# Self-edges of a graph counted with 25-column matmuls, and the 13 edge rows of histogram and ranking unrolled

## The reference

```python
x = x + attention(layernorm(x), rows=src, cols=dst)     # softmax over the edges of each src
x = x + experts(layernorm(x))
# graph attention: for each dst, softmax over its edges; one more self-edge per node is appended
src2 = concatenate([src, arange(n)]); dst2 = concatenate([dst, arange(n)])
h = gelu(gat(gelu(gat(layernorm(x), W0, src2, dst2)), W1, src2, dst2))
x = x + h; x = x + gated_experts(layernorm(x))
```

## Time and profile before

| | us |
|---|---|
| median of 3 runs | 4101.75 (4097.06 to 4112.96) |
| the profiled execution | 4131.15, its span 4129.2 |
| table "s": block A, B, C | 116 to 261, 261 to 410, 411 to 633 |
| table "d": block A, B, C | 636 to 752, 753 to 904, 905 to 1128 |
| all that follows | 1131 to 4129 |

### The profile page before, as it was taken

One profiled execution on the slowest core, in us unless ns is written; L12 is line 12 of the kernel. 1 busy time (PEld: TensorE's weight loads), 2 busy tenths in 40 slices (PEclk: granted clock), 3 DMA queues, 4 the chain that ended last, 5 costly groups with the idle time before them and its releaser, 6 DMA issues. The chain is left out here.

```text
span 4129.2 us, 64690 instructions
## 1 busy us (share of the span) xinstructions
PE 2505.8 (61%) x14572; PEld 1764.4 (43%) x14586; DVE 2269.1 (55%) x6592; ACT 1371.1 (33%) x4015; POOL 1731.6 (42%) x1826
## 2 busy tenths in 40 slices
PE   7569587586835454563799954344444445434399
PEld 4348124461223333343699952233322333323288
DVE  7857798667947676766311123444445444445542
ACT  2215581246846676431244421000000100000144
POOL 1510600013056666652122246566654656665411
PEclk9579795788966677675799976776777776677789
DMA  5148300561086666632222223333443333444200
GB/s 173 39 90 195 120 14 3 136 149 63 13 250 195 191 194 185 185 109 64 68 77 76 77 63 99 105 108 105 111 104 83 94 104 108 110 110 99 77 26 18
DMA packets 260802, 432.61 MB, mean 105 GB/s; under 512 B 101193, under 2 KB 185744, under 8 KB 259832
## 3 DMA queue, kind: packets, MB, share of 16 engines
q0 software_dynamic: 92912, 316.02, 26.5%
q1 hardware_dynamic: 124824, 108.37, 10.1%
q10 hardware_dynamic: 42992, 7.34, 1.0%
HBM read 378.79 MB, written 52.78 MB: 105 GB/s over the span
## 5 line engine op out<-in xcount | busy, mean ns | idle before, releaser
L1275 PE MATMUL gt_part<-gt_wv,all_ident 128*128 128x260 f32 x1648 | 566.8, 504 | 750.7 <-DVE gt_wv L1104 657.4
L1025 POOL DMA_INDIRECT gt_rows<-h_rows,gt_idx x824 | 789.0, 958 | 505.2 <-DVE gt_wv L1104 269.9
L1275 PEld LDWEIGHTS gt_part<-gt_wv,all_ident 128*128 128x128 f32 x1648 | 394.2, 252 | 923.3 <-DVE gt_wv L1104 721.7
L1025 POOL DMA_INDIRECT att_rows<-kv_rows,att_idx x412 | 425.0, 1031 | 385.4 <-issue 176.3
L1275 PE MATMUL att_part<-att_wv,all_ident 128*128 128x264 f32 x824 | 332.0, 572 | 351.3 <-ACT att_wv L1229 203.3
L1275 PEld LDWEIGHTS att_part<-att_wv,all_ident 128*128 128x128 f32 x824 | 221.0, 283 | 462.2 <-issue 336.2
L1229 ACT ACTIVATE att_wv<-att_rows,att_wv 128x32 f32<-128x32 f32 x1504 | 341.9, 308 | 88.5 <-issue 60.4
L1104 DVE TENSOR_TENSOR gt_wv<-gt_rows,gt_exps 128x1040 f32<-128x1040 f32 (+1 forms) x224 | 260.7, 1164 | 77.6 <-ACT gt_exps L1224 49.5
L1224 ACT ACTIVATE gt_exps<-gt_score 128x20 f32<-128x20 f32 (+1 forms) x224 | 42.5, 190 | 743.1 <-issue 395.4
L1224 ACT ACT_TABLE_LOAD x57 | 73.1, 1283 | 544.5 <-issue 544.2
L1123 DVE TENSOR_TENSOR gt_acc<-gt_acc,gt_part 128x260 f32 x224 | 95.1, 425 | 224.5 <-DMA qkv_x_all<-in_x 109.2
(11 more groups left out here) (536 smaller groups left out, 5299.9 us busy)
## 6 DMA issues: line engine op xcount, KB each, us to landing
ex_w<-in_W SPq DMA_DIRECT2D x16, 1024.0 KB, 6.4
ixbs_parts_bc<-key_parts_s SPq DMA_DIRECT2D x14, 1024.0 KB
ixbs_parts_bc<-key_parts_s SPq DMA_DIRECT2D x28, 512.0 KB
ixbd_parts_bc<-key_parts_d SPq DMA_DIRECT2D x14, 1024.0 KB
ixbd_parts_bc<-key_parts_d SPq DMA_DIRECT2D x28, 512.0 KB
gt_rows<-h_rows,gt_idx POOLq DMA_INDIRECT x824
kv_rows<-qk_kv_all SPq DMA_DIRECT2D x5, 1440.0 KB, 8.4
y_rows<-ex_y POOLq DMA_DIRECT2D x55, 128.0 KB, 2.0
```

Of the source, the lines that this page charges most:

```text
L1025: pool.indirect_dma_start(out=rows[:, k, r, :], out_offset=None, in_=table, in_offset=bass.IndirectOffsetOnAxis(ap=idx[:, k, r:r + 1], axi ...
L1275: last = pe.matmul(part[:, k, 0:h * av], c.ident[:, :], wv[:, k, first_wv + r, :, :].rearrange("p h f -> p (h f)"), start=(r == 0), stop=( ...
```

## The change

- Self-edges: ACT alone makes the one-hot, 25 `Square` instructions over 416 elements each, one for a tile number, and then 13 `Relu` (a row each). PE multiplies `oh_lo` with it into `node_loops`, 32 matmuls of 25 columns a row, each row 4 rows (`LOOP_LAG`) behind the histogram and the last 4 after the class sums. DVE cuts the counts into two digits (`loop_digits`, 5 small steps). In both tables POOL multiplies the digits with the one-hot of tiles (2 instructions, 128x625), PE puts them in the order of the table with 50 matmuls into `loops_ps`, ACT copies to `g.loops`.
- The DRAM table `loop_rows`, its stores, its fill and all 50 gathers of L753 are gone, with their waits.
- Block A's and block B's loops over rows are written out, all addresses constant; `load_low`, `load_key` and one-hots for row 13 are gone. SP's loop is written out too.
- `LEAST_ROUNDS` goes from 16 to 28. The first tile's largest degree is 35, so no round changes; but `sure_chunks(4)` goes from 2 to 5, so `attend` issues 4 index loads at once, not 2 and then 2 after reading the list.

```diff
-                    with dve.Fori(0, EU) as u:
+                    for u in range(EU):
                         one_hots(dve, u, ohs)
@@ block A, vector, after oh_val
+                    if count_loops:
+                        dve.wait_ge(loops_summed, EU)
+                        step(dve.tensor_copy(loops_i[:, 0, :], node_loops[:, :]))
+                        step(dve.tensor_single_scalar(loops_i[:, 1, :], loops_i[:, 0, :], LOOP_DIGIT - 1, ALU.bitwise_and))
+                        step(dve.tensor_single_scalar(loops_i[:, 2, :], loops_i[:, 0, :], 8, ALU.logical_shift_right))
+                        step(dve.tensor_copy(c.loop_digits[:, :, :], loops_i[:, 1:3, :]))
+                        dve.tensor_scalar(c.loop_digits[:, 1, :], c.loop_digits[:, 1, :], float(LOOP_DIGIT), None, ALU.mult).then_inc(loops_cut, 1)
@@ gpsimd
-                    if count_loops:
-                        with pool.Fori(0, EU) as u:
-                            pool.tensor_tensor(oh_loop[...], g.hi_c[...], c.iota_b[...], ALU.subtract).then_inc(loop_off, 1)
...
                     pool.partition_all_reduce(mdeg[:, :], sdeg[:, :], P, RMAX).then_inc(maxed, 1)
+                    if count_loops:
+                        pool.wait_ge(loops_cut, 1)
+                    for k in range(2):
+                        pool.tensor_tensor(loop_val[:, k, :, :], oh_tile[:, :, :], c.loop_digits[:, k, :].unsqueeze(2).to_broadcast([P, NT, NT]),
+                                           ALU.mult).then_inc(loops_valued, 1)
+                    pool.wait_ge(loops_valued, 2)
@@ scalar
+                        for t in range(NT):
+                            act.activation(oh_loop[:, :, :, t], g.hi_c[:, :, :, :].rearrange("p u x q -> p u (x q)"), ACT.Square, scale=-1.0,
+                                           bias=c.iota_f[:, LOOP_TILE + t:LOOP_TILE + t + 1]).then_inc(loop_squared, 1)
+                        act.wait_ge(loop_squared, NT)
+                        for u in range(EU):
+                            act.activation(oh_loop[:, u, :, :], oh_loop[:, u, :, :], ACT.Relu, scale=-1.0, bias=c.ones[:, 0:1]).then_inc(loop_ohs, 1)
...
+                    act.wait_ge(loops_placed, 1)
+                    act.activation(g.loops[:, :], loops_ps[:, :], ACT.Copy).then_inc(loops_ready, 1)
@@ tensor
+                    def loop_row(u):
+                        pe.wait_ge(loop_ohs, u + 1)
+                        for t in range(XC):
+                            last = pe.matmul(node_loops[:, :], oh_lo[:, u, t, :], oh_loop[:, u, t, :], start=(u == 0 and t == 0),
+                                             stop=(u == EU - 1 and t == XC - 1), skip_group_check=True)
+                        last.then_inc(loops_summed, 1)
-                    with pe.Fori(0, EU) as u:
+                    for u in range(EU):
                         pe.wait_ge(ohs, u * 2 + 2)
                         row(u)
+                        if count_loops and u >= LOOP_LAG:
+                            loop_row(u - LOOP_LAG)
@@ block B
-                row(0, 0, 0, True)
-                with eng.Fori(0, EU // 2) as i:
-                    for k in (1, 2):
-                        row(i * 2 + k, k % 2, i, False)
+                for u in range(EU):
+                    row(u, u % 2, u == 0)
...
-                            if x == 1:
+                            if x == 1 and u < last_u:
                                 low_one_hots(1 - uk, u + 1)
@@ block C, gpsimd
-                    for t in range(NT):
-                        pool.indirect_dma_start(out=g.loops[:, t:t + 1], out_offset=None, in_=loop_rows,
-                                                in_offset=bass.IndirectOffsetOnAxis(ap=g.order[:, t:t + 1], axis=0)).then_inc(loops_in, 16)
```

More of the change, by code:

```diff
@@ L425, in _ @@
                     act.wait_ge(lanes_set, 1)
[L426 to L431, removed]
+                    act.wait_ge(loops_placed, 1)
+                    act.activation(g.loops[:, :], loops_ps[:, :], ACT.Copy).then_inc(loops_ready, 1)
+                    act.wait_ge(loops_ready, 1)
                 @block.tensor
                 def _(pe):
[L435 to L448, removed]
+                    def loop_row(u):
[4 more added lines that the diff above has]
+                        last.then_inc(loops_summed, 1)
                     for b in range(2):
@@ L470, in _ @@
                     if count_loops:
-                        loop_rows(0, FIRST_LOOP_ROWS)
+                        for u in range(EU - LOOP_LAG, EU):
+                            loop_row(u)
                     pe.wait_ge(valued, 3)
@@ L477, in _ @@
                     last.then_inc(sums, 1)
-                    if count_loops:
-                        loop_rows(FIRST_LOOP_ROWS, EU)
-                        pe.wait_ge(loops_copied, 1)
-                        for t in range(EX):
-                            last = pe.matmul(loop_sums[:, :], c.ident[:, t * LOOP_TILE:t * LOOP_TILE + NT], loops_sb[:, t, :], start=(t == 0), stop=(t == EX - 1))
-                        last.then_inc(loops_joined, 1)
+                    pe.wait_ge(loops_valued, 2)
+                    for t in range(NT):
+                        for k in range(2):
+                            last = pe.matmul(loops_ps[:, :], oh_lane[:, t, :], loop_val[:, k, t, :],
+                                             start=(t == 0 and k == 0), stop=(t == NT - 1 and k == 1))
+                    last.then_inc(loops_placed, 1)
         with Mem(nc, f"ixb{g.name}") as b:
@@ L547, in _ @@
                                  entry[0:TAIL, 1, :]).then_inc(list_out, 16)
[L548 removed]
+                    for r in range(last_u):
                         sp.wait_ge(ohT_ready, r * 2 + 1)
[L550 removed]
+                        load_low(r + 1)
                         sp.wait_ge(ohT_ready, r * 2 + 2)
[L552 to L553 removed]
+                        load_key(r + 1)
                     sp.wait_ge(list_out, wins * 16 + 32)
                     sp.sem_inc(g.passed, 1)
[L556 to L557 removed]
                 @block.scalar
@@ L562, in _ @@
                     act.sem_inc(earlier_ready, 2)
-                    with act.Fori(0, EU) as u:
+                    for u in range(EU):
                         for x in range(EX):
@@ L624, in sum_places, with row @@
                                           pick[:, k, :, :, :].rearrange("p q r t -> p (q r) t"), AX.X, ALU.add).then_inc(reduced, 1)
-                    def row(u, uk, i, first):
+                    def row(u, uk, first):
                         for x in range(EX):
@@ L640, in _ @@
                     key_one_hots(0, 0)
-                    row_loop(dve, row)
+                    each_row(row)
                     for x in (2, 3):
```

56 lines of the change are left out of this document (16 added, 40 removed).

## The result

The kernel after takes 3977.44 us (median of 4 runs, 3973.43 to 3980.92) against 4102.26 (4097.06 to 4112.96): a ratio of 0.9692, 95% interval 0.9671 to 0.9714, 124.8 us less. I had forecast 3982.

What follows compares the result with a forecast made beforehand. Bounds: DVE in block A of "s", PE and DMA near their limits in B, DVE shut out by POOL's gathers in C. Savings 31.8 + 4.0 + 17.6 + 33.7 + 33.1 = 120; 4101.75 - 120 = 3982 us, range 3950 to 4032.

Steps and rivals of the forecast that it cites:

- Block A: One-hots, histogram and self-edges of each table: rows without POOL's work beside DVE; 31.8 us saved in "s", 4.0 in "d".
- Block B: Rows written out: PE gets faster, then the single-buffered key load holds a row at 9.35 us; both tables save 17.6.
- (d): Written-out PE code: supply of instructions makes PE pause, 224 us lost at 7 a pause, time 4206; chance 0.02.
- idle time by issue inside the written-out rows: Sign on PE in block B's rows: if it shows, the prediction is wrong.
- my bounds of 8.5 and 10 us: Sign in block B: a row under 8.5 or over 10 us would make the prediction wrong.
- the 1.00 that I had named: Sign in block B: PE's clock stays at 1.00 although PE idles 2 us a row.
- rival (c): Block B: an idle PE lowers its clock, -38 us in place of +7, total 75 saved, time 4027; chance 0.07.
- Block C: Tiles beside POOL: unbroken gathers of L753 starve DVE; removing them saves 33.7 us in "s", 33.1 in "d".
- (e): Block C is not held by POOL, so removing gathers saves nothing there; 53 us left, time 4049; chance 0.02.
- The rest: Earlier index loads in attend, stores, fill and semaphores: nothing saved, at most 1 us in each of three stages.
- The 29 us: Whole kernel: the profiled execution stood 29 us above the median, carried over unchanged into the forecast.

Runs made afterwards that it cites:

- a_no_self: Kernel after without any counting of self-edges, the counts set to zero in both tables: 3975.98 us, 0.9673 of before.
- the ring: Kernel after with block B's key digits loaded in halves into three half buffers, further ahead: 3619.45 us, 0.9773 of before.
- a_pool_beside: Kernel after with 13 subtractions of 1024 elements put back on POOL at the start of block A of "s": 3653.48 us.
- a_again: Kernel after, unchanged, on the other kind of chip: 3632.93 us against 3704.69 for the kernel before there, ratio 0.9807.
- the run with pauses: Kernel before, all work kept, POOL waiting after every fifth of the 25 self-edge gathers until they have landed: 0.9854 of before.
- b_again: Kernel before, unchanged, run once more for a second profile: 4095.54 us.

## Why the prediction was right

**Block A.** Cause, place and size were right: 33.2 to 33.3 of 31.8 in "s", 5.1 to 5.9 of 4.0 in "d". Several terms were off inside. ACT's `Square` I bounded by half of DVE's 0.98 us; it took 47.50 / 25 = 1.90 us, against 0.95 for 800 contiguous elements at L427 and 1.06 for 1024 in the `Square` of the kernel before. That is beyond the 1 us at which I said it would be late, and it was, by 21 us. What saved the sum was a slack I had also mis-sized: PE needs 1.7 us for a histogram and a loop row together and DVE 5.24 for one-hots, so PE regains 3.5 us a row, not "over 1". I had allowed 2 us for a histogram row at the lower clock; it takes 1.03 at a granted clock of 0.50. POOL's multiplies cost DVE 1.1 in "s" (the two scans 1.47 for 0.45, and small change), not 2.1. And the wait for the class sums grew from 2.35 to 3.10 us, which I had not counted. It isn't the loop row that now stands ahead of them, for `a_no_self` has no loop rows and waits 3.1 too. The second 25 of these matmuls take 2.87 us for 2.12: the granted clock was 0.72 over them before (us 223.5 to 225.7), after a histogram that had kept PE busy 7.58 of 8 us, and is 0.50 now (us 194.9 to 197.8), after 2.79 of 7.

**Block B.** Forecast 17.6, found 20.2 to 21.2. The mean row (low one-hots to low one-hots, ten rows) is 9.02 in "s" and 9.43 in "d"; I had taken 9.35. Before it is 9.7 to 9.9 on that count, a little over the 9.64 I took from ten rows. The last row went from 15.6 to 10.7 (352.76 to 363.49); the forecast had 10.1. The reason was right for "s": freed of the single buffer, a row falls from 9.16 to 8.52. For "d" it was half of it. Behind the key load stood a second limit of the same height, PE's pauses, most likely for code, which the ring brought onto the path: 9.31 without it, 9.54 with it. In the shadow of the key load they cost nothing: block B of "d" takes 143.2 us in `a_pool_beside` with 16.0 us of PE idle by "issue" in it, and 143.1 in `a_again` with 5.2.

I had put (d) at 0.02 as a loss of 224 us. Of my own signs, "idle time by issue inside the written-out rows" did appear (up to 2.4 us), without the time being wrong: that sign asked about a mechanism, not about its place on the path. Single rows also left my bounds of 8.5 and 10 us, from 8.30 to 10.25 behind the first; only their means kept to them. And the granted clock was 0.88 over rows of "s" (us 240 to 350) and 0.86 over those of "d", not the 1.00 that I had named, so what rival (c) feared happened a little, without a loss that shows: before it was 0.92. The Trainium skill, "Runtime: NRT & Kernel Launch", section "Instruction fetch mechanics", has straight code fetched ahead and mostly hidden, and a taken branch as what costs; here the loops' branch cost 0.4 to 0.5 us in two rows and the straight code, if the pauses are its, 2 to 3 us a pause beside full DMA engines.

**Block C.** Forecast 33.7 and 33.1, found 29.2 to 30.4 and 35.6 to 41.8. In "s" I took 2.03 tiles a us beside the own gathers and had 1.9; in "d" 1.8, and had 2.4. The reading of the windows, unbroken gathers starve DVE, is shown by the run with pauses, with one correction: they do so only from some 5 to 7 us on. What I could not see in one trace is that it holds on one kind of chip only: the forecast of 3982 was one for the kind that it was made from, and 0.981 instead of 0.969 is what the other gives.

I had read the Trainium skill, "SBUF — State Buffer", section "Who interferes with whom", as speaking for (e), because it names GpSimd's descriptor writing as starved by DVE. The same section also says that of these two engines the one that issues first gets the shared ports for its whole instruction and blocks the other, and that either can come out slower; so it doesn't speak against DVE as the loser. Whether the one-hots of block C use these ports no run shows. The traces have both: a gather of L753 takes 0.94 us beside a starved DVE and mostly 1.08 beside a busy one, and DVE was the one that stopped. Who issues first can't be read from them.

**The rest.** "Nothing" was right for loads and stores. But between attend and the experts all profiles of before-like kernels have 8 us that the after-like ones lack. Timelines of `b_again` and of after:

```profile
1926.42 0.16 POOL L1374 IOTA rt_node_f<- 128x25 f32 x1 [58.62 <-issue]
1926.62 0.19 DVE L1393 TENSOR_TENSOR rt_diff<-rt_top 128x25 f32<-128x25 f32 x1 [8.05 <-POOL rt_node_f L1374]
```
```profile
1796.58 0.17 POOL L1358 IOTA rt_node_f<- 128x25 f32 x1 [50.99 <-SPq L1355]
1796.79 0.19 DVE L1377 TENSOR_TENSOR rt_diff<-rt_top 128x25 f32<-128x25 f32 x1 [0.72 <-POOL rt_node_f L1358]
```

DVE waits for one small instruction of POOL, which waits for nothing. It is 7.8 to 8.7 us late in the six profiles of before and its variants, on time in after and six of its variants, and 7.7 late again in `a_no_self`, whose edit to POOL is two multiplies less and a memset more in each table, half a program ahead. I see no cause in the traces. An instruction packet starts inside the gap of `b_again` (us 1920.0), but in three of the seven late traces none does. That the place of the code decides is a guess from `a_no_self`; whatever does, nothing in the change aims at it, and 7.3 us of the gain are luck. They come on top of the 124.2 in the tables; against `b_again` the other stages behind the tables took 14 us away again.

**The 29 us** that I carried over were right to carry: they lay in stages that the change leaves alone, apart from 6 in block C of "d".

## What to carry to other kernels

Before a stage that is bound by VectorE, look at what GpSimd issues beside it: a pause after every few indirect gathers won back most of what removing them did (49 of 65 us in blocks C), and where DVE wasn't starved, even a pause after each of them cost nothing. When a loop is written out to free one engine, ask for the limits behind it one after the other, the load's buffer cycle and then the supply of code, and check idle time without a cause even where it is not on the path. Compare stages, not only totals: on a total of 4000 us a change of 20 can drown, and single profiles of one kernel differed by up to 13 in stages that nobody touched.

## What the runs showed of the hardware that I had not expected

- VectorE beside back-to-back gathers: 2 tiles in 10 us on one kind of chip, after 5 to 7 us at full rate; on another kind 24 in 10 us, beside 15 gathers without a pause. What differs stays open.
- Straight PE code beside DMA engines at a share of 0.77 to 0.90: pauses of up to 3.4 us, at worst nine of over 1 us in a block of 13 rows of about 390 matmuls. Looped: 0.4 to 0.5 per two rows.
- A single GpSimd instruction 8 us late in some builds and not in others, by nothing that the traces show.
- ScalarE: 1.90 us for a `Square` of 416 elements written with a stride of 25, 1.06 us for one of 1024 contiguous ones.
- PE: 32 pairs of weight load and 25-column matmul in 1.03 us with constant addresses, 5.05 with addresses from a register, both at a granted clock of 0.50.
